# Attention of an audio tower on one core: products in batches of four tiles, head pairs rounded as 128 rows and placed by DMAs

## The reference

```python
xn = _ln(x, ln_scale)
Q, K, V = (jnp.einsum('bse,hef->bhsf', xn, W) for W in (W_q, W_k, W_v))
q2 = jnp.sum(Q * Q, axis=-1)[..., :, None]
k2 = jnp.sum(K * K, axis=-1)[..., None, :]
qk = jnp.einsum('bhsf,bhtf->bhst', Q, K)
sqdist = jnp.maximum(q2 + k2 - 2.0 * qk, 0.0)
scores = jnp.exp(-gamma * sqdist)
out = jnp.einsum('bhst,bhtf->bhsf', scores, V)
return out.transpose(0, 2, 1, 3).reshape(B, S, H * E) @ W_o.T
```

## Time and profile before

| | us |
|---|---|
| median of 3 runs | 781.77 (781.49 to 782.96) |
| the profiled execution | 780.84 |
| its span, first to last instruction | 778.6 |

### The profile page before, as it was taken

One profiled execution on the slowest core, in us unless ns is written; L12 is line 12 of the kernel. 1 busy time (PEld: TensorE's weight loads), 2 busy tenths in 40 slices (PEclk: granted clock), 3 DMA queues, 4 the chain that ended last, 5 costly groups with the idle time before them and its releaser, 6 DMA issues.

```text
span 778.6 us, 16797 instructions
## 1 busy us (share of the span) xinstructions
PE 742.9 (95%) x5712; PEld 431.7 (55%) x5712; DVE 630.1 (81%) x1534; ACT 533.1 (68%) x1053; POOL 457.0 (59%) x620
## 2 busy tenths in 40 slices
PE   2999999999999999999999999999999999999994
PEld 1444356666667666666666666544555555454441
DVE  8676778888888888888888887788888888888864
ACT  1566779888888889888898888554554655555441
POOL 7644324544446454554546442367788788888885
PEclk9999999999999999999999999999999999999997
DMA  6200202211221112211221112000000000000000
GB/s 195 86 3 1 56 1 55 46 35 31 56 56 29 41 42 55 56 28 38 47 56 41 34 38 54 2 2 1 9 12 12 8 8 8 9 16 7 9 7 21
DMA packets 22620, 25.47 MB, mean 33 GB/s; under 512 B 12520, under 2 KB 21480, under 8 KB 22408
## 3 DMA queue, kind: packets, MB, share of 16 engines
q1 hardware_dynamic: 21544, 23.14, 12.7%
q10 hardware_dynamic: 992, 1.26, 0.6%
HBM read 5.06 MB, written 2.43 MB: 10 GB/s over the span
## 4 chain that ended last, share of the span: by engine, by line
PE 69%; POOL 10%; DVE 8%; ACT 5%; issue 4%; DMA 2%; SPq 0%; ACTq 0%; POOLq 0%; DVEq 0%
PE bank L1391 14%; PE bank L1369 13%; PE bank L1264 9%; PE bank L1222 8%; PE bank L1135 5%; PE bank L1288 5%; PE bank L1290 4%; DVE m L855 3%; POOL xn L429 2%; POOL inv L420 2%; PE bank L1125 2%; ACT prob L624 2%; POOL inv L412 1%; DVE prob L901 1%; ACT sq L588 1%
## 5 line engine op out<-in xcount | busy, mean ns | idle before, releaser
L440 POOL TENSOR_TENSOR sq<-sq 125x256 f32<-125x256 f32 x128 | 97.4, 772 | 162.2 <-ACT sq L588 139.5
L901 DVE TENSOR_SCALAR prob<-prob,cap_hi,cap_lo 125x500 f32<-125x500 f32 x256 | 156.1, 636 | 41.2 <-ACT prob L624 39.7
L624 ACT ACTIVATE prob<-bank 125x500 f32<-125x500 f32 x256 | 148.2, 591 | 34.9 <-PE bank L1290 32.5
L1369 PE MATMUL bank<-cs,w_sb 64*64 64x500 f32 x1024 | 147.0, 580 | 2.2 <-DVE gated L1019 2.0
L1391 PE MATMUL bank<-gated,w_sb 64*64 64x500 f32 x1024 | 148.7, 588 | 0.0
L482 POOL TENSOR_TENSOR gated<-relu,wb 128x500 f32<-128x500 f32 x96 | 119.9, 1250 | 48.2 <-ACT relu L722 45.7
L1019 DVE SCALAR_TENSOR_TENSOR gated<-bank,nb,wb 128x500 f32<-128x500 f32 x160 | 114.9, 727 | 35.2 <-PE bank L1369 35.2
L722 ACT ACTIVATE relu<-bank,b_sb 128x500 f32<-128x500 f32 x96 | 64.6, 673 | 93.2 <-PE bank L1369 93.2
L1369 PEld LDWEIGHTS bank<-cs,w_sb 64*64 64x64 f32 x1024 | 53.1, 133 | 54.7 <-issue 48.1
L1222 PE MATMUL bank<-wqku_hi,s 128*125 128x512 f32 x192 | 78.2, 407 | 2.8 <-DVE s L836 1.2
L588 ACT ACTIVATE sq<-bank 125x512 f32<-125x512 f32 x128 | 75.2, 598 | 8.2 <-PE bank L1222 4.7
(11 more groups left out here) (188 smaller groups left out, 1569.0 us busy)
## 6 DMA issues: line engine op xcount, KB each, us to landing
m1e<-m1e SPq DMA_DIRECT2D x64, 125.0 KB, 2.3
m1o<-m1o SPq DMA_DIRECT2D x64, 125.0 KB, 2.3
out<-res SPq DMA_DIRECT2D x15, 125.0 KB
w_sb<-in_w SPq DMA_DIRECT2D x1, 1024.0 KB
xa<-xparts SPq DMA_DIRECT2D x3, 281.2 KB
w_sb<-in_w SPq DMA_DIRECT2D x1, 512.0 KB
xw<-xparts SPq DMA_DIRECT2D x3, 140.6 KB
xparts<-x_part SPq DMA_DIRECT2D x3, 125.0 KB, 3.2
```

The costliest lines, as they stand in the source:

```text
L440: gp.tensor_tensor(sq2[q][:, :, :], sq[q][:, :, 0:D // 2], sq[q][:, :, D // 2:D], ALU.add)\
L624: act.activation(prob[v % PROBS][:, :, c, :], bank[5 + n % 3][0:T, 0:C].rearrange("p (h l) -> p h l", h=2), ACT.Exp).then_inc(b_exp, 1)
L901: dve.tensor_scalar(part, part, cap_hi[0:T, h:h + 1], cap_lo[0:T, h:h + 1], ALU.min, ALU.max)\
L1369: last = pe.matmul(up_bank(g)[cols, 0:C], w1_sb[rows, g, cols], cs1[q % 3][rows, :], start=True, stop=True)
```

## The change

Products are done in two batches of four tiles: after slot 0 tiles 4 to 7 of the pair before, after slot 4 tiles 0 to 3. So that six tiles may be alive, PROBS is 6, and buffers are numbered through all pairs.

From pair 1 on, a head group is rounded by one ScalarE instruction of 128 rows into a tile `mtop` of its own (two of the third stage's buffers `cs1`, under another type), and the remainder goes by one VectorE instruction of 128 rows into a tile `mlow`. SP places them (`spread`): four DMAs take each head's rounded rows to both halves of m1, two take the remainders to m2. Pair 0 keeps the old way. New waits keep ScalarE and VectorE from overwriting a tile whose DMAs are under way.

GpSimd does the first four of its seven scale steps before it waits for the norms.

```diff
+            def spread(p, j, u):
+                sp.wait_ge(b_ev, 16 * p + 9 + 2 * u)
+                wait(sp, b_sc, 16 * (p - 1))
+                for a in range(2):
+                    for rows in (slice(0, 64), slice(64, 128)):
+                        sp.dma_start(f32(m1[j][rows, 2 * u + a, :]), f32(mtop[u % 2][64 * a:64 * a + 64, :]))\
+                            .then_inc(b_dup[u], 16)
+                sp.wait_ge(b_gl, 4 * p + u + 1)
+                for a in range(2):
+                    sp.dma_start(f32(m2[j][0:64, 2 * u + a, :]), f32(mlow[u % 2][64 * a:64 * a + 64, :]))\
+                        .then_inc(b_low[u], 16)
+
             def duplicate(p, j, u):
+                if p > 0:
+                    spread(p, j, u)
+                    return
...
@@ GpSimd @@
                         gp.tensor_tensor(sq2[q][:, :, :], sq[q][:, :, 0:D // 2], sq[q][:, :, D // 2:D], ALU.add)\
                             .then_inc(b_sum, 1)
+                    if ln:
+                        first_scales(p + 1)
                     gp.wait_ge(b_red, 8 * p + 8)
...
                 if ln:
-                    b_scales(p + 1)
+                    second_scales(p + 1)
...
@@ ScalarE @@
-                if is_g(k):
-                    wait(act, b_sc, 16 * (p - 1))
+                if is_g(k) and p > 0:
+                    u = (k - 8) // 2
+                    wait_spread(act, p, u)
+                    act.wait_ge(b_gl, 4 * p + u - 1)
+                    act.activation(mtop[u % 2][:, :], src[:, 0:C], ACT.Copy).then_inc(b_ev, 1)
...
-                    wait(act, b_pv, 8 * (p - 1) + v - 3)
-                    act.activation(prob[v % PROBS][:, :, c, :], bank[5 + n % 3][0:T, 0:C].rearrange("p (h l) -> p h l", h=2),
+                    wait(act, b_pv, 8 * (p - 1) + v + 1 - PROBS)
+                    act.activation(prob[(8 * (p - 1) + v) % PROBS][:, :, c, :], bank[5 + n % 3][0:T, 0:C].rearrange("p (h l) -> p h l", h=2),
...
@@ VectorE @@
+                if p > 0:
+                    u = (k - 8) // 2
+                    wait_low(dve, p, u)
+                    dve.tensor_tensor(mlow[u % 2][:, :], src[:, 0:C], f32(mtop[u % 2][:, :]), ALU.subtract)\
+                        .then_inc(b_gl, 1)
+                    return
...
@@ TensorE @@
                     if v < 4 and c == 0:
-                        pe.wait_ge(b_gl, 4 * (p - 1) + hp + 1)
-                        pe.wait_ge(b_dup[hp], 32 * p)
+                        pe.wait_ge(b_dup[hp], spread_count(p - 1))
+                        if p == 1:
+                            pe.wait_ge(b_gl, hp + 1)
+                        else:
+                            pe.wait_ge(b_low[hp], 32 * (p - 1))
...
-                    for n in (v - 2, v - 1) if v % 2 == 0 else ():
+                    for n in range(4) if v % 4 == 0 else ():
                         for hh in range(2):
                             if v == 0 and old2:
-                                products(p - 2, n + 8, j, hh)
+                                products(p - 2, n + 4, j, hh)
                             if v > 0 and old:
                                 products(p - 1, n, o, hh)
...
-                    for n in (6, 7):
+                    for n in range(4, 8):
...
-PROBS = 4
+PROBS = 6
```

More of the change, by code:

```diff
@@ L150, in build @@
             ("xw", 1, [128, PAIRS // 2 * C], BF16))
-        m1e, ue, s2e, sq, sq2, m1o, uo, s2o, prob, y_att = phase(
+        m1e, ue, s2e, sq, sq2, m1o, uo, s2o, prob, y_att, mlow = phase(
             ("m1e", 1, [128, H, C], F32R), ("ue", 1, [T, CH, H * D], F32), ("s2e", 1, [S_ROWS, C], F32R),
@@ L156, in build @@
             ("m1o", 1, [128, H, C], F32R), ("uo", 1, [T, CH, H * D], F32), ("s2o", 1, [S_ROWS, C], F32R),
-            ("prob", PROBS, [T, 2, 2, L], F32), ("y_att", 2, [128, L], F32))
+            ("prob", PROBS, [T, 2, 2, L], F32), ("y_att", 2, [128, L], F32), ("mlow", 2, [128, C], F32R))
         m1, u_sb, s2 = m1e + m1o, ue + uo, s2e + s2o
+        mtop = [cs1[j].bitcast(F32R) for j in range(2)]
         relu_sb, gated, (y_moe,), (y_low,), (y_high,), (yt,), (yh,), (stats2,), (yz,), (res,), (y_fg,), (h_fb,), (res_last,), \
@@ L183, in build @@
         b_dup = [sem(f"b_dup{u}") for u in range(4)]
+        b_low = [sem(f"b_low{u}") for u in range(4)]
         b_qkw, b_qt, b_rnd2, b_s2, b_row = (sem(n) for n in ("b_qkw", "b_qt", "b_rnd2", "b_s2", "b_row"))
@@ L285, in wait_scratch, with spread_count, wait_spread, wait_low @@
             eng.wait_ge(a_ones, 1)
+        def spread_count(p):
+            return 32 + 64 * p
+        def wait_spread(eng, p, u):
+            if u >= 2:
+                eng.wait_ge(b_dup[u - 2], spread_count(p))
+            elif p > 1:
+                eng.wait_ge(b_dup[u + 2], spread_count(p - 1))
+        def wait_low(eng, p, u):
+            if u >= 2:
+                eng.wait_ge(b_low[u - 2], 32 * p)
+            elif p > 1:
+                eng.wait_ge(b_low[u + 2], 32 * (p - 1))
         block = ctx.enter_context(nc.Block())
@@ L403, in centred, with first_scales @@
                     .then_inc(s_out, 1)
-            def b_scales(p):
+            def first_scales(p):
                 n = 7 * p
@@ L416, in b_scales, with second_scales @@
                 gp.tensor_tensor(inv[:, 3, :], inv[:, 2, :], inv[:, 1, :], ALU.mult).then_inc(b_inv, 1)
+            def second_scales(p):
+                n = 7 * p
                 gp.wait_ge(b_inv, n + 4)
@@ L433, in step_b @@
                 if p == 0:
-                    b_scales(0)
+                    first_scales(0)
+                    second_scales(0)
                 if new:
@@ L579, in unit @@
                 act.wait_ge(b_pj, 16 * p + k + 1)
-                if is_g(k):
-                    wait(act, b_sc, 16 * (p - 1))
+                if is_g(k) and p > 0:
[3 more added lines that the diff above has]
+                    act.activation(mtop[u % 2][:, :], src[:, 0:C], ACT.Copy).then_inc(b_ev, 1)
+                elif is_g(k):
                     for a in range(2):
@@ L671, in tokens_c @@
                 act.wait_ge(c_xt, q + 1)
+                if q < 2:
+                    act.wait_ge(b_dup[q + 2], spread_count(PAIRS - 1))
                 act.activation(cs1[q % 3][:, :], bank[2][:, 0:C], ACT.Copy).then_inc(c_s1, 1)
@@ L899, in caps @@
                     dve.wait_ge(b_exp, 16 * (p - 1) + 2 * v + 2)
-                    part = prob[v % PROBS][:, hh, :, :]
+                    part = prob[(8 * (p - 1) + v) % PROBS][:, hh, :, :]
                     dve.tensor_scalar(part, part, cap_hi[0:T, h:h + 1], cap_lo[0:T, h:h + 1], ALU.min, ALU.max)\
@@ L1264, in products @@
                     last = pe.matmul(bank[1][64 * c:64 * c + 64, 0:L], u_sb[jj][:, 2 * b + c, h * D:(h + 1) * D],
-                                     prob[v % PROBS][:, hh, c, :], start=h == 0, stop=h == H - 1)
+                                     prob[(8 * p + v) % PROBS][:, hh, c, :], start=h == 0, stop=h == H - 1)
                 if hh == 1:
```

## The result

The changed kernel takes 821.58 us (median of four, 820.92 to 822.97) against 782.29 us (also of four, 781.49 to 782.96) for the kernel before: a ratio of 1.0495, 95% interval 1.048 to 1.051. It is slower, as forecast, but by 39.3 us and not by 10.7, and outside the range. Its profiled execution has a span of 819.0 us, 40.4 more than the 778.6 before.

What follows compares the result with a forecast made beforehand. TensorE, nearly full, was taken as the bound. 15 times -0.45 (T0 to X), 14 times +1.05 (X to T0), step 1 -0.34 and step 16 +3.04 gave +10.7 us: 792.5 us, range 780.5 to 804.

Steps and rivals of the forecast that it cites:

- The batch of slot 2: Two-tile batch of products on TensorE after slot 2 of a step; its removal was to save 2.03 us.
- the six issues: SP queue issuing six head-copy DMAs one after another at 0.566 us each, 3.40 us per head group.
- X to T0: From a step's first score to its slot 5's first score; 16.16 us before, forecast +1.05 a step.
- s1 to give back 0.30: TensorE's wait for VectorE's s1 at a step's first projection was to vanish behind the longer batch, -0.30 us.
- The pause before X: TensorE idle some 1.8 us before the next step's first score, waiting for the DMAs of the norm rows.
- the copies keep up: Four groups' copies, 15 us of issue a step, were to land before their scores, covered at nothing.
- nothing backs up: Against the rival of copies backing up on the queue: row DMAs landing 1 us later, 807 us; chance 0.07.
- the file: Six copy issues queued on SP ahead of the two norm-row DMAs, so the second row DMA issues at T0 + 5.97.
- T0 to X: From slot 5's first score (T0) to the next step's first score (X); 8.72 us before, forecast 8.27.
- TensorE's order and its short gaps set the step: Bound in a steady 24.84 us step: TensorE 24.66 us busy; ScalarE or VectorE savings count only where TensorE waits.
- The ends: First and last attention steps: step 1 was to change by -0.34 us, step 16 by +3.04.
- Worth nothing by itself: One 128-row rounding saves ScalarE and VectorE four instructions a pair each; forecast no gain, since neither is the bound.

## Why the prediction was wrong

Three terms of the sum failed. The batch of slot 2 was taken out at its own 2.03 us, though it also covered the squares (0.7 us a step); pauses were priced at their length, though the clock fell behind some (11.4 us in all); and the six issues were taken at 3.40 us and measured 3.80.

**Right: the batches and the wait for the rows.** Four tiles instead of two were to cost X to T0 1.69 - 2.03 + 1.69 = 1.35 us, and s1 to give back 0.30. Two-tile steps measure 15.81 (16.1 before), four-tile steps without other losses 17.15: 1.34 and 0.3. The pause before X, its cause and its place were forecast too: 1.8 us, measured 2.0. That the copies keep up as long as their order stays is right; the runs with the rows first show how little room there is. Landings were 2.25 us with three times the bytes, so nothing backs up.

**Mis-sized: the file.** T0 to X was to be 8.27 and is 8.67, 15 x 0.40 = 6 us. SyncE's start at T0 + 1.85 and the landing of 2.25 are as forecast; the difference is the six issues, 3.80 us from first issue to the rows' (3.75 with the scales back, where VectorE is not late) and not 6 x 0.566 = 3.40. One in file takes 0.60 to 0.62, with 0.04 to 0.12 between groups; the row of 0.566 was of two.

**Missed: the squares.** I costed the batch of slot 2 by its own time alone and named no chain that it covers, while I did so for slot 6. It gave the squares their time: X to T0 is 17.93 and not 17.2, about 0.7 x 14 = 10 us. "TensorE's order and its short gaps set the step" is where this failed: a gap-free TensorE also hides how near the others are.

**Missed: the clock.** The sum took pauses at their own length. A pause of 2 us also let the clock fall, in six of 14 steps, 9.7 us more than 14 steps of 26.61, and in the last batch of step 16 once more: after a wait of 2.55 us for wtok (the gate weights) it takes 5.28 us at a granted clock of 0.67, where in the run with filling and four squares buffers the same batch, after 2.58 us, takes 3.59 at 1.00.

**The ends.** From X of step 16 to the experts 27.42 us against 22.49: +4.9 where +3.04 was forecast; 1.7 of the difference is that batch, and without it (the same run) it is +3.2.

**The sum.** 10.7 forecast, 6 (file), 10 (squares), 9.7 + 1.7 (clock), and 1.7 by which the first X is late in this execution (109.10 against 107.37, before anything that was changed runs; it lies between 107.9 and 110.7 in the other runs): 39.8 of 40.4. Step 1 waits for the squares too, another 0.7 (X to T0 13.81, where the forecast has 13.44 - 0.34 = 13.10). So the terms meet the total within a few tenths.

"Worth nothing by itself", said of the 128-row rounding, was not run alone. With two-tile batches the whole rest of the change leaves the time as it was; with four-tile batches and the old rounding TensorE waits 1.2 us a step for ScalarE.

Left open: why the same pause lowers the clock once and not the next time, and why always with four squares buffers. The runs show only that behind X it stays at 1.00 in all steps when the pause is filled.

## What to carry to other kernels

Where the bound engine is full, look at each of its long pieces not for its cost but for what it covers: before you merge or move one, list the chains of the other engines that end behind it, and what is late when it is gone. A pause costs more than its length if the clock falls behind it, and a saving elsewhere can be eaten by that, so undo causes together as well as one by one. Small DMAs that a bound engine waits for belong on a queue with nothing in front of them; changing the order of a full queue made something else late here.

## What the runs showed that was not expected

- Pauses of 1.9 to 2.4 us on TensorE were followed by a granted clock of about 0.6 for some 4 us in six of 14 steps, and in 14 of 14 with four squares buffers, where X to T0 holds no wait for the squares.
- Two caps of VectorE took 2.39 us instead of 0.98 while GpSimd ran hc, z and xn on tiles of 256 and 512 elements; 0.98 (in the run with the scales back) while it ran mostly small ones, and there a single cap beside xn took 1.13 (at 319.68). The Trainium skill, "GPSIMD Engine Reference", section "1. Specifications", says that GpSimd shares its SBUF interfaces with VectorE, with contention for VectorE's instructions in a 2-port mode or with two SBUF inputs. The rows agree in that the caps take longer beside GpSimd's larger steps; in which mode the caps run no row shows.
- Two DMAs issued from ScalarE's queue, 0.63 and 0.66 us each, ran beside its activations (345.18 beside 345.05 and 345.52 above), without a gap in them up to ScalarE's wait for TensorE. What they cost a ScalarE that has no such wait behind them, no run shows.
